# Conditioning experts of two layers: tile products from two-part splits in place of full precision

## The reference, cut to what matters

```
hidden = gelu(x @ W1[e])        # 256 -> 256
y      = hidden @ W2[e]         # 256 -> 256
```

## Time and profile before

| | |
|---|---|
| median of 3 runs | 1671.27 us (1671.03 to 1673.64) |
| profiled execution, its own time | 1685.24 us |
| its span, first to last instruction | 1683.5 us |
| granted TensorE clock, mean share of full speed | 0.931 |
| busy: PE, its weight loads, DVE, ACT, POOL | 87%, 66%, 58%, 39%, 25% |
| the tiles of layer 2 | from 501 to 596 us |
| the tiles of layer 3 | from 1344 to 1439 us |

### The profile page before, as it was taken

One profiled execution on the slowest core, in us unless ns is written; L12 is line 12 of the kernel. 1 busy time (PEld: TensorE's weight loads), 2 busy tenths in 40 slices (PEclk: granted clock), 3 DMA queues, 4 the chain that ended last, 5 costly groups with the idle time before them and its releaser, 6 DMA issues. The chain is left out here.

```text
span 1683.5 us, 25908 instructions
## 1 busy us (share of the span) xinstructions
PE 1471.8 (87%) x8350; PEld 1117.3 (66%) x8350; DVE 984.0 (58%) x1754; ACT 656.8 (39%) x977; POOL 428.6 (25%) x366
## 2 busy tenths in 40 slices
PE   7886888765989998798999999999979899759994
PEld 5632334733877787687888888887867777636663
DVE  5665676335644364735777776775646333447665
ACT  3366775213233332424655555553332233211110
POOL 0612231000433410010233443332004334113331
PEclk9999999955899999999999999999998999859997
DMA  5378972252222240240221322201313222355743
GB/s 178 110 289 323 335 250 100 99 195 101 88 100 88 92 153 1 88 175 4 98 101 31 113 86 104 100 23 33 121 33 117 101 86 91 119 209 166 251 147 122
DMA packets 82918, 211.38 MB, mean 126 GB/s; under 512 B 10785, under 2 KB 57762, under 8 KB 74594
## 3 DMA queue, kind: packets, MB, share of 16 engines
q1 hardware_dynamic: 66944, 166.40, 27.6%
q0 software_dynamic: 15840, 43.27, 7.7%
q10 hardware_dynamic: 2, 0.00, 0.0%
HBM read 165.21 MB, written 44.43 MB: 125 GB/s over the span
## 5 line engine op out<-in xcount | busy, mean ns | idle before, releaser
L633 POOL DMA_INDIRECT results<-sb_big,sb_s_out_row x63 | 134.2, 2130 | 452.8 <-ACT sb_big L864 298.1
L938 DVE TENSOR_TENSOR sb_h_split<-sb_big,sb_h_split 128x2048 fp32r<-128x2048 f32 x78 | 178.5, 2289 | 87.1 <-ACT sb_h_split L933 87.1
L933 ACT CAST sb_h_split<-sb_big 128x2048 fp32r x78 | 146.6, 1903 | 34.2 <-issue 32.9
L829 PE MATMUL ps<-sb_big,sb_e_hT 128*128 x624 | 141.0, 379 | 1.1 <-DVE sb_e_hT L986 1.1
L1078 ACT COPY sb_g_space<-sb_big 128x1024 f32 x120 | 118.7, 1050 | 47.5 <-DMA sb_big<-in_l_routed 23.5
L320 PE MATMUL ps<-sb_h_split 128*128 128x512 f32 x312 | 133.1, 426 | 3.8 <-issue 2.8
L1078 DVE COPY sb_g_space<-sb_big 128x1024 f32 x168 | 108.1, 698 | 47.3 <-DMA sb_big<-in_l_routed 21.8
L829 PEld LDWEIGHTS ps<-sb_big,sb_e_hT 128*128 128x128 f32 x624 | 118.2, 190 | 18.5 <-issue 1.3
L1479 POOL DMA_INDIRECT sorted_in<-sb_big,sb_p_slots x64 | 70.2, 1097 | 222.7 <-DVE sb_p_slots L1304 167.4
L322 PE MATMUL ps<-sb_h_split 128*128 128x512 f32 x312 | 123.9, 397 | 0.0
L321 PE MATMUL ps<-sb_h_split 128*128 128x512 f32 x312 | 123.6, 396 | 0.0
(11 more groups left out here) (450 smaller groups left out, 3193.3 us busy)
## 6 DMA issues: line engine op xcount, KB each, us to landing
sb_big<-in_l_routed SPq DMA_DIRECT2D x32, 1024.0 KB
sb_big<-in_l2f_routed SPq DMA_DIRECT2D x8, 3072.0 KB, 10.6
sb_e_wring<-in_l_experts SPq DMA_DIRECT2D x16, 1408.0 KB
sb_big<-in_l_routed SPq DMA_DIRECT2D x32, 512.0 KB
sb_big<-results SPq DMA_DIRECT2D x32, 512.0 KB, 7.5
sb_big<-sorted_in SPq DMA_DIRECT2D x18, 512.0 KB
by_token<-sb_big SPq DMA_DIRECT2D x12, 512.0 KB, 4.2
sorted_in<-sb_l1p_zero SPq DMA_DIRECT2D x2, 2048.0 KB, 9.6
```

The costliest lines, as they stand in the source:

```text
L633: pool.indirect_dma_start(out=results, out_offset=bass.IndirectOffsetOnAxis(ap=places.out_row[:, j:j + 1], axis=0), in_=self.tile(j), in_o ...
L829: last = pe.matmul(psum[:, 7, 0:D], self.hT[:, f // TPC, f % TPC * P:(f % TPC + 1) * P], self.weight(place, 2 * KD * self.F + f * D, D), s ...
L933: act.copy(self.own[part][:, 0, :], self.raw(e, part)).then_inc(self.own_high[part], 1)
L938: dve.tensor_tensor(self.own[part][:, 1, :], self.raw(e, part), self.own[part][:, 0, :], ALU.subtract).then_inc(self.own_low[part], 1)
```

## The change

The class of the tiles is replaced by `SplitGeluExperts`, in both layers.

- Each product is made of `matmul_split`s: rows, hidden tiles and weights exist as high and low part, so a product of two float32 matmuls becomes six fp32r matmuls.
- ACT makes the high parts (rows, hidden, weights), DVE the low ones. ACT now copies the transposed hidden tile, DVE subtracts. The low weights overwrite the loaded ones (`rounded` lies over the same SBUF); the high ones and the split rows and hidden tiles lie in the split buffer of the jobs.
- The weights of the first four experts are split before the first tile: by ACT once the last up part of the jobs is done, by DVE as `closing`. The other four are split in tiles 0 to 3. Tile `j` needs the weights of at most `j + 1` experts.
- The transposed rows have two PSUM banks instead of one, and PE transposes them two tiles ahead instead of one.
- In layer 2 the second unit's weights are split in tiles 6 to 11 instead of 0 to 5.
- `glu.resume` is set: the features of the first job after the tiles are split after the last down product, no longer in the first part.

```diff
+            sb("lower_part", [P, FCOL], on=place)
+            rounded = sb("rounded", [P, 2 * NT * D], F32R, on=place)
...
-        class GeluExperts:
+        class SplitGeluExperts:
             NF = 2
+            HELD = 4
...
+                self.high = glu.split[:, 0:E2 * self.W].rearrange("p (e n) -> p e n", e=E2)
+                self.rT, self.hT = (glu.split[:, lo:lo + 4 * D].rearrange("p (n h t) -> p n h t", n=2, h=2)
+                                    for lo in (E2 * self.W, E2 * self.W + 4 * D))
...
+            def weight_high(self, act, e):
+                if e == 0:
+                    act.wait_ge(self.loaded, 16)
+                act.copy(self.high[:, e, :], self.raw[:, e, :]).then_inc(self.w_high, 1)
+            def weight_low(self, dve, e):
+                dve.wait_ge(self.w_high, e + 1)
+                dve.tensor_tensor(self.low[:, e, :], self.raw[:, e, :], self.high[:, e, :], ALU.subtract).then_inc(self.w_low, 1)
...
+            def product(self, pe, to, e, left, lo):
+                for k in range(KD):
+                    at = lo + k * D
+                    last = matmul_split(pe, to, [left[:, h, k * P:(k + 1) * P] for h in range(2)],
+                                        [w[:, e, at:at + D].rearrange("p s n -> p (s n)") for w in (self.high, self.low)],
+                                        k == 0, k == KD - 1)
+                return last
             def up_product(self, pe, j):
                 e = self.expert_of(pe, j)
-                pe.wait_ge(self.rows_c, j + 1)
+                pe.wait_ge(self.w_low, min(j + 1, E2))
+                pe.wait_ge(self.rows_l, j + 1)
                 if j >= 2:
-                    pe.wait_ge(self.raw, j - 1)
...
+                    pe.wait_ge(self.raw_h, j - 1)
+                self.product(pe, psum[:, j % 2, 0:D], e, self.rT[:, j % 2, :, :], 0).then_inc(self.up, 1)
...
             def pe_tiles(self, pe):
-                pe.wait_ge(self.loaded, 16)
                 self.turn_rows(pe, 0)
+                self.turn_rows(pe, 1)
                 for j in range(self.tiles):
                     self.up_product(pe, j)
                     if j >= 1:
                         self.turn_hidden(pe, j - 1)
-                    if j + 1 < self.tiles:
-                        self.turn_rows(pe, j + 1)
+                    if j + 2 < self.tiles:
+                        self.turn_rows(pe, j + 2)
...
             def act_tiles(self, act, between=None):
-                self.copy_rows(act, 0)
+                self.rows_high(act, 0)
+                self.rows_high(act, 1)
                 for j in range(self.tiles):
...
                     act.wait_ge(self.up, j + 1)
...
+                    if j + self.HELD < E2:
+                        self.weight_high(act, j + self.HELD)
+                    if j >= 1:
+                        self.hidden_high(act, j - 1)
+                    if j + 2 < self.tiles:
+                        self.rows_high(act, j + 2)
+                    if between is not None:
+                        between(j)
...
             def dve_tiles(self, dve, between=None):
-                self.copy_hidden(dve, 0)
+                self.rows_low(dve, 0)
+                self.rows_low(dve, 1)
                 for j in range(self.tiles):
+                    if j + self.HELD < E2:
+                        self.weight_low(dve, j + self.HELD)
+                    if j >= 1:
+                        self.hidden_low(dve, j - 1)
+                    if j + 2 < self.tiles:
+                        self.rows_low(dve, j + 2)
+                    if j >= 2:
+                        self.result(dve, j - 2)
...
+                glu.resume = split
...
                         glu.act_jobs(act, 0, split)
-                        experts.act_tiles(act, lambda j: glu.weights_high(act, 1, j) if two and j < 6 else None)
+                        experts.act_open(act, wait_space)
+                        act.wait_ge(glu.downed, 2 * split)
+                        experts.act_tiles(act, lambda j: glu.weights_high(act, 1, j - 6) if two and 6 <= j < 12 else None)
+                        act.wait_ge(experts.downed, experts.tiles)
+                        glu.features_high(act, split)
...
-                        glu.dve_jobs(dve, 0, split, beside=trace)
+                        glu.dve_jobs(dve, 0, split, beside=trace, closing=lambda: experts.dve_open(dve))
+                        dve.wait_ge(glu.downed, 2 * split)
                         route.gates_of(dve, link, 2 * scale if two else scale)
...
+                        glu.features_low(dve, split)
```

More of the change, by code:

```diff
@@ L70, in build @@
         XTOK, ACC, FCOL, CTOK, FCOL2, EXTRA = (n * NT * D for n in range(6))
+        with ExitStack() as place:
+            sb("lower_part", [P, FCOL], on=place)
+            rounded = sb("rounded", [P, 2 * NT * D], F32R, on=place)
         big = sb("big", [P, 6 * NT * D])
@@ L659, in turn_rows @@
             def turn_rows(self, pe, j):
                 self.rows.wait_landed(pe, j)
-                if j >= 1:
-                    pe.wait_ge(self.rows_c, j)
+                if j >= 2:
+                    pe.wait_ge(self.rows_l, j - 1)
                 for k in range(KD):
-                    last = pe.transpose(psum[:, 6, k * P:(k + 1) * P], self.rows.tile(j)[:, k * P:(k + 1) * P], ident[:])
+                    last = pe.transpose(psum[:, 6 + j % 2, k * P:(k + 1) * P], self.rows.tile(j)[:, k * P:(k + 1) * P], ident[:])
@@ L690, in down_product @@
                 e = self.expert_of(pe, j)
-                pe.wait_ge(self.hid_c, j + 1)
+                pe.wait_ge(self.hid_l, j + 1)
                 if j >= 2:
                     pe.wait_ge(self.outc, j - 1)
[L694 to L699, removed]
+                self.product(pe, psum[:, 2 + j % 2, 0:D], e, self.hT[:, j % 2, :, :], KD * D).then_inc(self.downed, 1)
             def pe_tiles(self, pe):
-                pe.wait_ge(self.loaded, 16)
                 self.turn_rows(pe, 0)
+                self.turn_rows(pe, 1)
                 for j in range(self.tiles):
@@ L720, in copy_rows, with hidden_high, act_open @@
                     act.wait_ge(self.up, j - 1)
-                act.copy(self.rT[:, j % 2, :], psum[:, 6, 0:D]).then_inc(self.rows_c, 1)
+                act.copy(self.rT[:, j % 2, 0, :], psum[:, 6 + j % 2, 0:D]).then_inc(self.rows_h, 1)
+            def hidden_high(self, act, j):
+                act.wait_ge(self.hid_t, j + 1)
+                if j >= 2:
+                    act.wait_ge(self.downed, j - 1)
+                act.copy(self.hT[:, j % 2, 0, :], psum[:, 4 + j % 2, 0:D]).then_inc(self.hid_h, 1)
+            def act_open(self, act, wait_space):
+                for e in range(self.HELD):
+                    wait_space(act)
+                    self.weight_high(act, e)
             def act_tiles(self, act, between=None):
-                self.copy_rows(act, 0)
+                self.rows_high(act, 0)
+                self.rows_high(act, 1)
                 for j in range(self.tiles):
-                    if between is not None:
-                        between(j)
                     act.wait_ge(self.up, j + 1)
@@ L1648, in half_cond, with wait_space @@
                 closing = range(max(split, N - 2), N)
+                def wait_space(eng):
+                    eng.wait_ge(glu.both, glu.NF * split)
                 with nc.Block() as block:
```

58 lines of the change are left out of this document (30 added, 28 removed).

## The result

| | before | after |
|---|---|---|
| median | 1672.45 us (4 runs, 1671.03 to 1673.74) | 1726.84 us (4 runs, 1718.10 to 1728.05) |
| ratio, 95% interval | | 1.031 (1.028 to 1.035) |
| span of the profiled execution | 1683.5 us | 1726.3 us |

The account below looks back on a forecast made before the run. PE's sequencer was taken to bound the expert tiles. 25.3 us per layer, 50.6 in both, on the profiled 1685.24 us gave 1735.8; the runs' median lying 14 us lower, the forecast was 1722 us, range 1702 to 1760.

Parts of the forecast that it names:

- The bound: Expert tiles before the change: PE's sequencer fills the 2.30 us of an undisturbed tile, the array close behind at 2.16 us.
- these four numbers fill the tile: Tile before: 14 sequencer instructions (1354 ns), 8 matmuls, 54 ns gap each and 24 ns per matmul make up 2.30 us.
- Array: PE array per tile: 12 split matmuls and 4 transposes take 1.88 us, alone giving 0.28 us per tile back.
- Sequencer: PE's sequencer per tile: low slices 96 ns, repeated slices 24 ns, 240 ns per product, +0.48 us per tile.
- Rival A: Expert tiles: every matmul recomputes its address, tile 3.35 us, kernel 1757 us; chance 0.17.
- B: Expert tiles: the array, not the sequencer, is the bound, so faster: tile 1.94 us, kernel 1658 us; chance 0.05.
- C: Tile loop: the clock falls to 1.2 GHz and the array becomes the bound, kernel 1784 us; chance 0.04.
- with the same 0.06 us of disturbance: Mean over the tiles: 2.78 us undisturbed becomes 2.84; 34 tiles against 2.36 us cost +16.3 us per layer.
- ACT, DVE and the first weights at nothing: ACT's 1.13 and DVE's 1.27 us per tile, and splitting the first four weights before the tiles, cost zero.
- Opening: Start of the tiles: low rows queue behind DVE's gates, and up product 2 waits for weight 4; +5.0 us per layer.
- Closing: Last tiles to next job: late features cost +2.7 us, the lowered clock after that gap +1.3 us, per layer.
- The sum: Per layer 5.0 + 16.3 + 2.7 + 1.3 = 25.3 us, both layers 50.6 us.

Follow-up runs that it names:

- static experts: The changed kernel with each tile's expert fixed in the program (tile number modulo 8), no number loaded, no address computed: 0.990 times the kernel before, tile 1.87 us.

## Why the prediction was right

**The bound.** Right, and shown. One load less moves the tile from 2.91 to 2.15 us, no loads and addresses to 1.87, and an assert at every use to 3.12 where one load had 2.15, all with the same products. Of two runs that each take four matmuls per tile from the array, the one that takes no address with them changes the tile by 0.08 us, the other by 0.57. The reading of before that carried it was that the sequencer's intervals add up to the tile. One step of that reading proved less than it said: the gap of 54 ns and the 24 ns per matmul were solved from the tile of 2.30 us, so that "these four numbers fill the tile" held by construction. Two things could have gone against it and did not: the trace's own gaps (18 ns of assert to 77, 51 ns of semaphore to 106) are 55 to 59 ns, and the 24 ns came out as 20 in the run without low rows.

**Array.** Said 1.88 us, measured 1.87 with static experts. Its gain of 0.28 us is real and stays hidden as long as the sequencer needs more.

**Sequencer.** Said +0.48 us per tile; the shortest tiles are 2.75 after 2.29 us in layer 2, +0.47, and 2.73 after 2.30 in layer 3, +0.43. The low weights have a one-operation address as assumed (32 ns, where I worked out 18; to the next instruction, the matmul behind it included, 112 and not 96) and the repeated high ones none. Rival A, an address for every matmul, did not come: eight address rows per tile, not twelve. B did not: PE idles in the tiles. C did not: the clock is 1.00 in the steady tiles.

**The mis-sized term** is the mean over the tiles: "with the same 0.06 us of disturbance". The tiles of 2.91 and 2.90 us lie 0.13 us above the undisturbed 2.78, so that 34 tiles cost 18.8 and 18.4 us and not 16.3. The table shows where most of it is: 0.09 us more in the two loads, 16 of which are stretched instead of 2. With four matmuls fewer 5 are (no low rows) or none (no low weights), so it goes with what is issued between the loads; why was not settled.

**ACT, DVE and the first weights at nothing.** Right: with static experts the same work fits a tile of 1.87 us, and the jobs take 46.15 us either way.

**Opening.** Said +5.0 us: +5.1 and +5.5. The order on DVE did most of it: moving the gates took 3.3 and 3.9 us of it back, the clock's share included.

**Closing.** Said 2.7 and 1.3: 2.7 and 1.6. The splitting of the features after the last product causes it; given a place of their own, layer 2 loses nothing. That the clock fell in both layers was partly luck: of the 18 closings with late features in all these traces it did not fall in 5.

**The sum.** 25.3 us per layer forecast, 28.2 in the table; both layers 50.6 against 54.4 by the medians. No term was too high to cover for another: all lie at or a little under what came. My remark that the profiled execution lay 14 us above the median mattered: by its span alone the change would seem to cost 43 us.

## What to carry to other kernels

Where an engine's matmuls have addresses from a register, add up its sequencer's rows (load, range check, assert, address, semaphore, each from start to the next start) before counting passes on the array: here cheaper arithmetic cost 3%, two thirds of it because it needed more addresses, and one load less per tile was worth as much as the whole change lost. Load an index once with its range stated and keep the register for every use; leaving the range out cost an assert per use. Where two limits lie close, mix the forms (one product split, one not) until both are equal, and ask of every moved chain of small instructions (the gates) whether the work behind it has become urgent.

## What the runs showed of the hardware

- A matmul whose address is ready takes the sequencer 20 ns (0.08 us for four), an assert of 18 ns takes 77 ns to the next instruction, an address of 32 ns with its matmul 112.
- A load of the expert takes 0.35 us to the next instruction at best; with two per tile in the split version up to 0.77.
- After nearly the same idle time of PE (2.4 to 2.6 us) the clock fell in some executions and not in others: the 47 matmuls behind it took 12.4 us in both layers of the changed kernel, but 10.7 to 10.8 us in layer 3 of three experiments and in layer 2 of two others. A term like the closing's 1.3 us is a chance, not a constant.
- In the profiled execution of the kernel before, matmuls of layer 3's jobs that otherwise start 0.12 us apart started 0.7 to 1.9 us apart with nothing awaited, which with the lowered clock behind them cost 8.7 us. Five of twelve experiments have such pauses, all on two of four chips, in code that the others run without them. The cause is open.
